# Attention and FFN layer on one core: split halves, a new order of the steps, another prologue and end

## What is computed

```python
qkv = x @ Wqkv + bqkv
# blocks of 128 queries see the blocks before, of, and after them; |kpos - qpos| <= 128
scores = where(mask, q @ k.T / 16, -1e30)
out = (softmax(scores) @ v) @ Wout + bout
x = layernorm(x + out)
Wq = clip(round(W / (mean(abs(W)) + 1e-5)), -1, 1)      # for W1 (1024 x 256) and W2
h = relu(x @ Wq1.T + b1)
x = layernorm(x + h @ Wq2.T + b2)
```

## Time and profile before

| | |
|---|---|
| median of 3 runs | 1175.44 us (1175.4 to 1178.41) |
| profiled execution | 1178.41 us, span 1176.7 us |
| PE busy | 973.5 us (83%), mean granted clock 0.904 |
| DVE busy | 813.6 us (69%) |
| ACT busy | 704.1 us (60%) |
| POOL busy | 612.6 us (52%) |
| chain that ended last | PE 47%, ACT 22%, DVE 14% |

### The profile page before, as it was taken

The page is one execution under the profiler, slowest core; times in us unless marked ns, Lnnn a source line. Parts: engine busy times, 40 slices in busy tenths (PEclk is TensorE's granted clock), DMA queues, the critical chain, the costliest instruction groups (busy, mean ns, idle before and its releaser), DMA issues.

```text
span 1176.7 us, 28808 instructions
## 1 busy us (share of the span) xinstructions
PE 973.5 (83%) x10628; PEld 772.5 (66%) x10628; DVE 813.6 (69%) x2900; ACT 704.1 (60%) x1401; POOL 612.6 (52%) x951
## 2 busy tenths in 40 slices
PE   4798887988798888979798898879888797977866
PEld 2474776766676676767577676767677676666644
DVE  3785868678685867768686767768686867866222
ACT  3254765849485665848476584848567584835613
POOL 1124464655656555655655466565645465554522
PEclk8587899989999898999899899989989998997967
DMA  8654334344452543454263434445254434431000
GB/s 194 71 87 74 48 64 81 60 80 74 75 91 38 93 64 73 66 92 74 58 92 55 81 61 79 75 79 86 39 95 63 81 57 74 74 61 33 11 9 18
DMA packets 58026, 81.82 MB, mean 70 GB/s; under 512 B 8736, under 2 KB 28704, under 8 KB 57888
## 3 DMA queue, kind: packets, MB, share of 16 engines
q1 hardware_dynamic: 57888, 79.99, 40.9%
HBM read 20.19 MB, written 8.39 MB: 24 GB/s over the span
## 4 chain that ended last, share of the span: by engine, by line
PE 47%; ACT 22%; DVE 14%; issue 9%; POOL 4%; DMA 2%; SPq 1%; DVEq 0%; ACTq 0%; POOLq 0%
PE shared L538 24%; PE st L500 8%; PE shared L586 7%; DVE mx L899 7%; ACT probs L749 6%; ACT hidden L825 5%; PE mx L516 5%; ACT hid_hi L828 4%; ACT x L807 2%; PE shared L558 2%; ACT oT_x1T_hi L813 1%; DVE rmax L899 1%; ACT qk_hi L773 1%; POOL probs L1059 1%; PE shared L599 1%
## 5 line engine op out<-in xcount | busy, mean ns | idle before, releaser
L899 DVE CUSTOM_DVE_ANT_0 mx<-mx,band 128x384 f32<-128x384 f32 (+1 forms) x1024 | 479.0, 517 | 250.4 <-PE mx L516 245.5
L749 ACT ACTIVATE probs<-st 128x384 f32<-128x384 f32 (+1 forms) x768 | 365.3, 524 | 186.8 <-PE st L500 183.6
L516 PE MATMUL mx<-k_stack,q_stack 48*128 48x384 f32 (+1 forms) x1024 | 290.7, 371 | 22.3 <-DVE rmax L899 17.2
L1059 POOL TENSOR_SCALAR_AFFINE_SELECT probs<-probs 128x512 f32<-128x512 f32 (+1 forms) x256 | 127.8, 524 | 311.0 <-ACT probs L749 311.0
L500 PE MATMUL st<-q_stack,k_stack 50*128 50x384 f32 (+1 forms) x1024 | 266.7, 355 | 12.3 <-ACT probs L749 7.0
L500 PEld LDWEIGHTS st<-q_stack,k_stack 50*128 50x128 f32 x1024 | 183.8, 209 | 63.7 <-issue 30.7
L516 PEld LDWEIGHTS mx<-k_stack,q_stack 48*128 48x128 f32 x1024 | 186.0, 210 | 50.0 <-DVE rmax L899 39.5
L586 PE MATMUL shared<-probs,v_aug 128*32 128x384 f32 (+1 forms) x2048 | 165.1, 448 | 9.4 <-POOL probs L1063 7.2
L538 PE MATMUL shared<-w2q,hid_hi 64*128 64x256 f32 x1024 | 158.3, 306 | 2.0 <-POOL hid_lo L1104 1.7
L538 PE MATMUL shared<-w2q,hid_lo 64*128 64x256 f32 x1024 | 150.2, 295 | 0.0
L899 DVE DVE_READ_ACCUMULATOR2_ANT rmax<- 128x1 f32 x1024 | 144.2, 141 | 0.0
(11 more groups left out here) (99 smaller groups left out, 1883.5 us busy)
## 6 DMA issues: line engine op xcount, KB each, us to landing
q_stack<-qk_hi SPq DMA_DIRECT2D x128, 128.0 KB, 4.2
k_stack<-qk_hi SPq DMA_DIRECT2D x128, 128.0 KB, 5.0
x_raw<-in_xT SPq DMA_DIRECT2D x16, 512.0 KB, 5.8
q_stack<-qk_lo SPq DMA_DIRECT2D x64, 128.0 KB, 3.9
k_stack<-qk_lo SPq DMA_DIRECT2D x64, 128.0 KB, 5.5
y<-in_x SPq DMA_DIRECT2D x16, 512.0 KB, 6.3
out<-x SPq DMA_DIRECT2D x32, 256.0 KB, 2.2
probs<-in_w2T SPq DMA_DIRECT2D x1, 1024.0 KB, 10.2
```

What stands on the lines that cost most here:

```text
L516: mm = pe.matmul(PMX[i % N_MAX][:, col:col + n], SQ[rows, hd, W * m:W * m + W], SK[rows, hd, k0:k0 + n], start=True, stop=True)
L749: act.activation(PR[:, v % 2, g // 2, lo:lo + n], PST[i % N_SCORE][:, 0:n], ACT.Exp, scale=SCALE) \
L899: mx = dve.tensor_tensor_reduce(ps, ps, band, 1.0, -3e38, ALU.add, ALU.max, RMAX[:, g, m:m + 1])
L1059: pool.affine_select(out=pr_before, in_=pr_before, compare_op=ALU.is_ge, fill=0.0, base=0, pattern=[[0, n], [1, W]], channel_multiplier=-1)
```

## The change

It rewrites the order of all queues, cuts side steps in two, and changes prologue and end; what is computed for each row stays the same.

- `SIDE`: each step in two halves is now two entries, ("start", step) for the first half and the step itself for the second, and both may have other steps between. `qk 0`, `vp` move to quad 0, `ot` and `op` behind `qk 0`; `ut` of quads 2 and 3 is done a step or more later. The transposes of `ot`, the matmuls and their number are as before.
- Units: instead of runs of two pairs, each scores unit and each maxima unit has its own place (`SCORES_AT`, `MAXIMA_AT`, in thousandths of the quad's side work).
- ACT gets an order of its own with lags (`ACT_LAG`), DVE lags per step (`DVE_LAG`).
- FFN1's lo parts: one of eight blocks on POOL (`REST_ON_POOL = (3,)`), in the last row none; `x1` of tile 0 on DVE.
- Bank pairs are given out as they come free; stacks are issued as soon as their hi parts are there; store order follows `ln2`.
- Prologue: 28 small matmuls on the identity ahead of all; the weights other than Wqkv are loaded behind the second stack; sums and thresholds move to the start of `at = 0`; quantising is in eight chunks of 512 columns, two by DVE and six by POOL. In `at = 0` and the later half of `at = -1` dummy matmuls stand where `op`, `f1` and `f2` have no row yet.
- End: dummy matmuls ahead of `op`, `x1t` and `f1 0` in the last call (`WARM_END`). For the middle rows the table `WARM` is empty.

The diff, cut to its core:

```diff
 SIDE = [
-    ["nmt", "pv", "ut", "ot", "op", ("ln1", 0), ("ln1", 1), ("ln1", 2), ("ln1", 3)],
-    [("qk", 0), ("x1", 0), ("x1", 1), "nmt", "pv", ("x1", 2), "ut", ("x1", 3), "x1t", ("qk", 1), ("f1", 0)],
-    [("f1", 1), "vp", ("f1", 2), ("f1", 3), "nmt", "pv", "ut", ("xs", 0), ("xs", 1)],
-    [("f2", 0), ("ln2", 0), "xr", ("ln2", 1), "nmt", "pv", "ut", ("f2", 1), ("ln2", 2), ("ln2", 3)],
+    [("start", "qk", 0), "nmt", "pv", ("ut", 0), ("qk", 0), ("start", "ot"), "ot", ("start", "vp"),
+     ("start", "op"), "vp", "op", ("ln1", 0), ("ln1", 1), ("ln1", 2)],
+    [("ln1", 3), ("x1", 0), ("start", "qk", 1), ("qk", 1), ("x1", 1), ("x1", 2), "nmt", "pv", ("x1", 3),
+     ("ut", 1), ("start", "x1t"), "x1t", ("start", "f1", 0), ("f1", 0), ("start", "f1", 1), ("f1", 1),
+     ("start", "f1", 2)],
+    [("f1", 2), ("start", "f1", 3), "xr", ("f1", 3), "nmt", "pv", ("start", "f2", 0), ("f2", 0)],
+    [("start", "f2", 1), ("ut", 2), ("xs", 0), ("f2", 1), ("xs", 1), "nmt", "pv", ("ut", 3), ("ln2", 0),
+     ("ln2", 1), ("ln2", 2), ("ln2", 3)],
 ]
...
-REST_ON_POOL = (0, 2, 4, 6)
-X1_ON_DVE = ()
-RUN = 2
-RUNS_AT = (0.95, 0.93)
+REST_ON_POOL = (3,)
+X1_ON_DVE = (0,)
+SCORES_AT = ((57, 63, 184, 334, 424, 487, 492, 504, 606, 632, 712, 872),
+             (0, 0, 19, 24, 31, 56, 76, 278, 457, 582, 699, 949),
+             (383, 483, 646, 667, 727, 730, 764, 766, 835, 920, 928, 995),
+             (0, 70, 95, 150, 234, 252, 259, 439, 460, 584, 659, 661))
+MAXIMA_AT = ((121, 126, 221, 289, 550, 575, 633, 708, 807, 844, 970, 995),
+             (109, 276, 313, 353, 380, 388, 600, 610, 645, 694, 782, 955),
+             (0, 59, 160, 188, 342, 528, 556, 668, 725, 762, 825, 944),
+             (0, 73, 215, 242, 259, 458, 566, 744, 755, 860, 862, 880))
...
+WARM = {}
+WARM_END = {("start", "op"): 4, ("start", "x1t"): 16, ("start", "f1", 0): 8}
+WARM_UP = 14
+FILLED = {"op", "f1", "f2"}
...
+def act_order(v):
...
+    for step, woven in zip(SIDE[v], WOVEN[v]):
+        lag = lag_of(ACT_LAG, step)
+        if lag < 0:
+            due(UNITS + 100)
+            out.append(("side", step))
+        for _, kind, i in woven:
+            if kind == "scores":
+                out.append(("exp", i))
...
+            def exchange(passed):
+                passed()
+                pe.wait_ge(s_half, halves[0])
+
+            def one_half(out, terms, filled, passed, second, ready=None):
+                count = len(terms[0])
+                if second:
+                    exchange(passed)
+                for n in range(count):
+                    if n > 0 or not second:
+                        passed()
+                    if ready is not None and not second:
+                        ready(n)
+                    for rows, k in ((LOWER, second), (UPPER, 1 - second)):
...
+            def warm(out, times, width=S):
+                for _ in range(times):
+                    for i, rows in enumerate((LOWER, UPPER)):
+                        pe.matmul(out[i][:, 0:width], WQKV[0][rows, 0, 0:P], WQKV[0][rows, 1, 0:width], start=True, stop=True)
...
+                        elif row is None and (at == 0 or at == -1 and v > 1) and name_of(whole(step)) in FILLED:
+                            cost, count = HALF_COST[name_of(whole(step))]
+                            out = pair_free(PAIR[at, v, step], b)
+                            for _ in range(count):
+                                passed()
+                                warm(out, 1, cost // count // 2)
...
+            def quantise(n):
+                raw, ternary, i = chunk(n)
...
+                pool.tensor_scalar(below, raw, THR[:, 2 + i:3 + i], None, ALU.is_lt).then_inc(s_below, 1)
+                pool.tensor_scalar(ternary, raw, THR[:, i:i + 1], None, ALU.is_gt).then_inc(s_above, 1)
...
+                pool.tensor_tensor(ternary, ternary.bitcast(F32), below.bitcast(F32), ALU.subtract).then_inc(s_quant_p, 1)
```

More of the change, by code:

```diff
@@ L126, in weave @@
-        slot = [[] for _ in SIDE[v]]
-        for n, i in enumerate(runs):
-            if n in place:
-                k, p = place[n]
-            else:
-                k = max(k for k, s in enumerate(SIDE[v]) if starts[k] <= where[n] and COST.get(name_of(s), (0, 0))[0])
-                cost, places = COST[name_of(SIDE[v][k])]
-                p = min(int((where[n] - starts[k]) / cost * places), places - 1)
-            slot[k] += [(p, kind, u) for u in range(i, i + RUN) for kind in ("scores", "max")]
@@ L138, in weave @@
+        out.append([sorted(((p, kind, i) for (kind, i), (k, p) in put.items() if k == n), key=lambda u: (u[0], u[1] != "scores", u[2]))
+                    for n in range(len(costs))])
+        for kind in ("scores", "max"):
+            assert [i for units in out[-1] for _, what, i in units if what == kind] == list(range(UNITS))
     return out
 PAIR = pairs()
+STORED_AFTER = [[(v, s) for v in range(QUADS) for s in SIDE[v] if s == ("ln2", 2 * h + 1)][0] for h in range(2)]
 WOVEN = weave()
@@ L204, in dve_order, with due @@
     return out
+def act_order(v):
+    out, late, exps = [], [], 0
+    def due(now):
+        while late and late[0][0] <= now:
+            out.append(("side", late.pop(0)[1]))
+    for step, woven in zip(SIDE[v], WOVEN[v]):
[6 more added lines that the diff above has]
+                out.append(("exp", i))
+                exps += 1
+                due(exps)
+        if lag >= 0:
+            late.append((exps + lag, step))
+            due(exps)
+    due(UNITS + 100)
+    return out
 def steps(step):
-    for row in range(-2, B + 1):
+    for row in range(-2, B + 2):
         step(row, row)
@@ L464, in _ @@
         def _(pe):
+            pe.wait_ge(s_ident, 1)
+            for _ in range(WARM_UP):
+                for i, rows in enumerate((LOWER, UPPER)):
+                    pe.matmul(PG[:, i, 0:P], IDN[rows, :], IDN[rows, :], start=True, stop=True)
             pe.wait_ge(s_const, CONSTANTS)
@@ new lines, in one_half @@
+                    for rows, k in ((LOWER, second), (UPPER, 1 - second)):
+                        cols, lhs, rhs = terms[k][n]
+                        mm = pe.matmul(out[k][:, cols], lhs(rows), rhs(rows), start=n == 0 and not second,
+                                       stop=n == count - 1 and bool(second), skip_group_check=True)
+                        if n == count - 1:
+                            mm.then_inc(filled if second else s_half, 1)
+                            halves[0] += not second
@@ new lines, in half_of_transposes @@
+            def half_of_transposes(out, block, filled, passed, second, ready=None):
+                if second:
+                    exchange(passed)
+                for t in range(TB):
+                    if t > 0 or not second:
+                        passed()
+                    if ready is not None and not second:
+                        ready(t)
+                    for rows, k in ((LOWER, second), (UPPER, 1 - second)):
+                        col = P * t + rows.start
+                        mm = pe.transpose(out[k][:, col:col + 64], block(rows, t, k), IDN[rows, rows])
+                        if t == TB - 1:
+                            mm.then_inc(filled if second else s_half, 1)
+                            halves[0] += not second
@@ L604, in side_work @@
                     c = step[1]
-                    if c == 0:
+                    if c == 0 and not second:
                         pe.wait_ge(s_xh, 2 * r + 2)
```

442 lines of the change are left out of this document (239 added, 203 removed), and 10 rows, old and new, of tables (ACT_LAG, DVE_LAG).

## The result

The changed kernel takes 1296.28 us (median, 1285.52 to 1315.02) against 1175.42 us of the kernel before on the same chip: ratio 1.100, 95% interval 1.089 to 1.112. The forecast was 1105 us.

What follows compares the result with a forecast made beforehand. No engine is full; PE's in-order queue and its waits set the row. Prologue 95.5 + 15 rows x 64.4 + end 44 + 1.7 = 1107, less 3: 1104, say 1105 us; range 1040 to 1165.

Steps and rivals of the forecast that it cites:

- my prices: PE's stream costs from instruction starts: 40.3 us side work plus 9.3 us for 96 paired units, 49.6 us a row.
- A: First stretch of a middle row, nmt to end of op: 16.4 us before, 17.9 forecast, PE waiting about 1.6.
- B: Second stretch of a middle row, end of op until FFN1 begins: 13.9 us before, 14.2 forecast, as a chain.
- C: Last stretch of a middle row, from FFN1's begin: 36.9 us before, 32.9 forecast, with 3.0 us of waits.
- In A that goes, in B it comes: The fall to half clock leaves A and comes in B, costing 1.3 us (bounds 0 and 1.65).
- M7 to M11: Maxima units 7 to 11 of a quad, behind the last pv in C: 3.0 us of DVE, 1.0 of stream.
- 6.2 less 1.9: Middle row: 64 units standing alone add 6.2 us of PE stream; the offset of array halves recovers 1.9.
- A's clock still falls: Sign of being wrong: the granted clock, forecast at 1.0 in A, still drops there.
- The slow rival: B's wait drops the clock, which stays down through FFN1: row 71.9 us, time 1218 us; chance 0.09.
- Nothing in the rows: The split saves nothing in middle rows, 67.2 us; only prologue and end gain: 1147 us (1135 to 1170); chance 0.22.
- Prologue: Before the middle rows: first u copy at 95.5 us instead of 114.0, first exp at 42, row 0 taking 49.
- End: After the middle rows: 44 us instead of 54.6, dummies holding the clock and FFN1 bound by ACT.

Runs made afterwards that it cites:

- a1_warm: The changed kernel with dummy matmuls in two waits of the middle rows, ahead of x1t and the first FFN1 pair: 1265.59 us, ratio 1.077.
- b1_unpaired: The kernel before with each maxima unit one place behind its scores unit, so every pair is broken: 1239.48 us, ratio 1.056.
- e3_adjacent: The changed kernel with its four parted steps brought together again: 1395.31 us, ratio 1.188.

## Why the prediction was wrong, point by point

**Where the row went wrong.** I forecast 67.20 - 2.8 = 64.4 and got 74.90. The forecast is an absolute sum, so it can be laid beside the ledger kind by kind, and so can the kernel before by the same prices:

| us a row | before, my prices | before, ledger | change, forecast | change, ledger |
|---|---|---|---|---|
| PE's work | 49.6 | 53.31 | 53.9 | 57.10 |
| half clock | 1.65 | 3.82 | 1.3 | 7.96 |
| waits | 15.95 (the rest) | 10.07 | 9.2 (the rest) | 9.84 |
| row | 67.2 | 67.20 | 64.4 | 74.90 |

The forecast's waits are 1.6 in A, 4.5 in B (14.2 less 9.7 of stream) and 3.0 in C, 9.1 together; the trace has 1.7, 4.8 and 3.2 in the example row. So the places where PE waits were foreseen. Of the 10.5 us that the row is over the forecast, 6.7 are the clock, 3.2 the work and 0.6 the waits.

**The clock: the step that failed.** "In A that goes, in B it comes", at 1.3 us a row, was right about B, at the place named, and far too small: 7.96 us a row. The fall in B lasted 9.5 us at 0.50 in the example row, not 3.3, and there were two more, in `qk 1` and behind the last `pv`, where I had priced PE's waits for M7 to M11 at 3.0 us and never asked what they do to the clock. The size of 3.3 us was read off a single row of the kernel before, which has one of the shorter falls; over 15 rows that kernel lost 3.82 us and not 1.65. Against the kernel before the clock costs 4.1 x 15 = 62 us. a1_warm shows that much of it can be taken back by filling two waits: the loss falls to 3.72 and the row to 71.68. The row before's 67.20 it does not reach, so the clock is not the whole cause.

**The work: prices too low, in both kernels.** My prices leave out 3.7 us of work in the row before and 3.2 in the row after. Since I set the new sum beside the measured 67.20, what was missing came out as a gain: the kernel before seemed to have 15.95 us of waits to win from, 3.7 of them unpriced work and 2.2 clock. The waits that were to fall by 6.75 us fell by 0.2. Added to the row after, the 3.7 us alone make it 68.1, +0.9 us, and the time about 1105 + 15 x 3.7 = 1160 us. The difference of the work, +3.8, was near the forecast +4.3 (6.2 less 1.9) by luck: a broken pair costs 0.055 us in b1_unpaired and not 0.193, and there is other work that I had not seen and still can't assign.

**Stretch by stretch.** A 20.1 (17.9): the waits for `o_norm` and `oT_lo` are gone, as forecast, the exp wait stands in `ot` (0.92 us at 668.65), waits in all 1.7 (1.6 forecast); the stretch begins at clock 0.61 with what the row before left, so "A's clock still falls", one of my signs of being wrong, came true in part. B 17.55 (14.2): the chain was the right view, its order of events as forecast, but the waits ahead of `ut 1` and FFN1 are 2.3 us together and not 4, the rest stands at M3, M4 and, for exps, in `qk 1`; it missed clock 0.79. C 37.45 (32.9): waits 3.2 (3.0 forecast), clock 0.91, of which I had nothing.

**The slow rival** had the mechanism (B's wait drops the clock, FFN1 runs at half speed until 700.9) and a row of 71.9, and got 0.09. I held against it that the clock came back after 3.3 us in A. In ten of the 15 rows it had taken 7 us or more there, so the objection rested on the row that I happened to read. The row's 71.9 was reached and passed with the help of the two other falls and of work that this rival did not have.

**"Nothing in the rows"** expected 67.2 us, and the row is 7.7 us longer. Whether the split pays for itself no run shows by itself: in e3_adjacent the units moved with it.

**Prologue: 138.0, forecast 95.5.** First maxima at 26.7 us (22.5). The two quads of maxima ended at 51.7 (38), from 32 us on at clock 0.50, PE full until 48: I had bounded them by DVE's pace. x's split came at 46.39, after 20.66 us of ACT waiting for x_raw, which I had not followed on the queue. First exp 55.57 (42). Row 0 82 us (49): "dummies, so the clock stays up" failed, it was 0.50 from 108 to 124 us. POOL's chunk of about 4.4 us lay within the bounds of 3.7 to 6.1; whether it held row 0 up was not tried. Up to 11 us of the 138.0 may be chance, since the same prologue gave 127.0 in another variant.

**End: 51.8, forecast 44.** FFN1 now runs at clock 1.00 (1276 to 1290 us), as forecast; -2.8 us and not -10.6. In the last 11.3 us PE is busy 2.4, so I take it that ACT's and DVE's pieces behind it set the end; no run tests it.
